# Joining the first pass's scatter with the second edge pass, in parts of 512 columns

## The chip, the cores and the metric

The kernel runs on one core of one Trainium2 chip. The metric is the device time of one execution in microseconds (us); lower is better.

## The reference

Four graph layers run one after another over the same 4096-node graph (`adj` 4096x4096, features 64 wide), each followed by a residual and a layer norm. The change touches the third, which runs the same layer twice (`it` 0 and 1):

```python
x = _layernorm(x + _L0_gnn_ref(x, adj, ...)); x = _layernorm(x + _L1_gnn_ref(x, adj, ...))
# third layer, twice, H = adj:
Q = x @ Wq + bq; V = x @ Wv + bv
edge_feat = H.T @ V                              # the "edge pass"
att = softmax(Q @ edge_feat.T * scale * H, axis=1)      # "attend"
...                                              # node and edge masks -> H_pruned
agg = (H_pruned.T * dv_isqrt[None, :] @ transformed) * de_inv[:, None]
msg = dv_isqrt[:, None] * (H_pruned @ agg)       # gather, then scatter
x   = relu(msg @ Theta)                          # the "messages"
# then a fourth layer with decaying weights
```

So the second pass begins with x = messages of the first: V = x @ Wv + bv needs them, and `H.T @ V` reads the whole matrix again.

## The kernel before

The matrix is handled as 32 row blocks of 128x4096 float32 (2048 KB). They stream from HBM into eight slots of on-chip memory (`slot`: six in `stream`, then `q2` and `x2`, which the trace calls query_twice and node_twice). All loads named here are issued by SyncE on one queue. Node features lie as [128, 32 blocks, 64]; a part is a quarter of that, 8 blocks or 512 columns.

The program is cut into phases by `phase(name)`. When a phase is left, all engines drain and meet (L172), GpSimd clears the phase's semaphores (L174), and all engines meet again (L175). Before the change there are two phases. `first_pass` holds `front` (the first two layers and the first edge pass), `attend` and `prune_and_sum` for it 0. `second_pass` holds `edge_pass`, `attend` and `prune_and_sum` for it 1, with the last layer.

`prune_and_sum` ends in eight groups of gather (L1658), aggregate (L1670) and scatter (L1686) on TensorE. After the last scatter, ScalarE (L1785) and VectorE (L1832) copy the sums from PSUM into `accT`, and TensorE makes the 32 messages (L1713) in two halves of 16, each over two parts; VectorE takes every part with relu and the node's factor (L1836). SyncE has meanwhile issued the loads of row blocks 0 to 7 of the next edge pass: two (L1613) and two (L1618) as slots fall free, and blocks 4 to 7 (L1621) when the scatter is done.

`edge_pass` then folds (transposes) all of x in 16 steps (L228), ScalarE copies the four parts back (L528), TensorE projects them by Wv (L215) and VectorE adds the bias (L534, `moved`). After that come the 32 edge blocks: block n is eight matmuls (L579) that add into PSUM banks 4 to 7. Between certain blocks stand other products (`beside`: features after block 6, queries after 9 and 11, and so on). SyncE reloads a place when its block was used (L554): block 8 goes where block 0 was, 9 where 1 was, 10 where 4 was, and from there six places take turns:

```python
def place(n):
    return n if n < 8 else (0, 1, 4, 5, 6, 7)[(n - 8) % 6]
```

`attend` copies the summed edge features out of PSUM (L1383 on VectorE, L1390 on ScalarE), then computes scores (L1140 on TensorE, L1175 on VectorE), exponentials on ScalarE and column sums (L1158). It begins when the semaphore of the last edge block says so, with no phase boundary ahead of it.

A matmul on float32 appears in the trace as two records, so an edge block of eight matmuls is 16 records.

Of the kernel before, what the change touches and what calls it, by code (L numbers as in the profile page):

```python
# [22 lines left out]
P = 128  # L23
# [65 lines left out]
def build(nc, d):  # L89
    ctx = ExitStack()  # L90
    with ctx:
# [417 lines left out]
        def edge_pass(block, sem, src, begun):  # L509
# [7 lines left out]
            features, query_first, query_second, _, _, fold_xn, nodes_first, nodes_second = side  # L517

            @block.tensor
            def _(pe):  # L520
                fold(src, fold4b, fold_ready)
                project(nat4, curT, wv, v_ready, before=lambda k: pe.wait_ge(fold_taken, k + 1))

            @block.scalar
            def _(act):
                for k in range(4):
                    act.wait_ge(fold_ready, k + 1)
                    nc.scalar.copy(bank_of(curT, k), bank_of(fold4b, k)).then_inc(fold_taken, 1)  # L528

            @block.vector  # L530
            def _(dve):
                for k in range(4):
                    dve.wait_ge(v_ready, k + 1)
                    nc.vector.tensor_tensor(part(moved, k), part(nat4, k), per_feature(bv, QB), ALU.add)\  # L534
                        .then_inc(v_taken, 1)
# [36 lines left out]

            return (used, NB)
# [115 lines left out]
        def front(block, sem):  # L689
# [390 lines left out]
            return (used, 4 * TILES + NB), (starts_stored, 16)  # L1080

# [281 lines left out]
        def attend(block, sem, it, edges_summed, edge_place_free):  # L1363
# [22 lines left out]
            def _(act):  # L1386
                for taken, value in (edges_summed, *edge_place_free):
                    act.wait_ge(taken, value)
# [4 lines left out]
            def _(sp):  # L1393
                sp.wait_ge(*edges_summed)
# [50 lines left out]
        def prune_and_sum(block, sem, it, scores_done, sums_done):  # L1445
# [108 lines left out]
            def place(n):  # L1554
                return (n + 8) % NB

# [67 lines left out]
            def _(pe):  # L1624
# [81 lines left out]

                pe.wait_ge(msg_taken, 4)
                for pair in ((24, 16), (0, 8)) if last_it else ((0, 8), (24, 16)):
                    for k in range(8):
                        for n in pair:  # L1710
                            h, m = divmod(place(n + k), 16)
                            at = 8 * TURN.index(n // 8) + k if last_it else n + k
# [183 lines left out]
```

## Time and profile before

| | |
|---|---|
| median of 3 runs | 2362.62 us (2361.77 to 2362.78) |
| the profiled execution, its own time | 2364.53 us |
| its span | 2362.6 us |
| mean granted TensorE clock | 0.944 of full |
| TensorE matmul busy | 2048.1 us (87%) |
| VectorE busy | 1727.4 us (73%) |
| ScalarE busy | 754.1 us (32%) |
| HBM traffic | 690.29 MB read, 136.31 MB written, 350 GB/s over the span |

The profiled execution's own time is 1.9 us over its span, and 1.9 us over the median of the runs. Times within the trace count from the start of the span. PEclk is the granted clock: 1.00 is 2.4 GHz, 0.50 is 1.2 GHz.

### The profile page before, as it was taken

The numbers are of one execution on the slowest core, as the hardware profiler recorded it, in microseconds if no ns is written. First come the engines' busy times: TensorE is split into PE (matmuls) and PEld (weight loads), VectorE is DVE, ScalarE is ACT, GpSimd is POOL, SyncE is SP. The second block draws the span as 40 slices with busy tenths as digits, with TensorE's granted clock in tenths as the row PEclk, the third lists the DMA queues.
The fourth block names the chain that finished last, engine by engine and source line by source line (L and its number), as shares of the span: only waits on it lengthen the run. The fifth ranks groups of instructions, "written<-read, shape, count | busy, mean of one in ns | idle before, by whom it ended". The sixth has DMA issues, their size and how long they took to land. (4 is left out here: it accounts for less than half of the span.)

```text
span 2362.6 us, 35866 instructions
## 1 busy us (share of the span) xinstructions
PE 2048.1 (87%) x15654; PEld 729.9 (31%) x15658; DVE 1727.4 (73%) x2056; ACT 754.1 (32%) x869; POOL 4.5 (0%) x18
## 2 busy tenths in 40 slices
PE   6899989899977777799999989987777689997997
PEld 2224333222322111234444323231212134344333
DVE  5996853188879999855541348879999965555998
ACT  0001000066634433211110026654433311112997
POOL 0000000000000000000000000000000000000000
PEclk9999999999988888799999999998888899998999
DMA  9988999999749999977779989938999987775994
GB/s 374 421 367 339 421 428 427 394 390 370 273 181 401 429 430 431 408 262 272 286 289 385 428 372 382 380 114 346 421 428 431 421 327 270 276 286 238 350 420 169
DMA packets 130219, 828.90 MB, mean 351 GB/s; under 512 B 8464, under 2 KB 10512, under 8 KB 76560
## 3 DMA queue, kind: packets, MB, share of 16 engines
q1 hardware_dynamic: 128016, 825.29, 86.7%
q8 instruction: 122, 2.00, 0.3%
q10 hardware_dynamic: 2048, 1.35, 0.2%
q14 instruction: 33, 0.27, 0.0%
HBM read 690.29 MB, written 136.31 MB: 350 GB/s over the span
## 5 line engine op out<-in xcount | busy, mean ns | idle before, releaser
L1185 ACT ACTIVATE stream<-stream,negmax 128x4096 f32<-128x4096 f32 x128 | 475.0, 3711 | 481.9 <-DVE negmax L1180 481.9
L1140 PE MATMUL ps<-edgeT,node_twice 64*128 64x512 f32 x1024 | 282.8, 672 | 156.3 <-DVE mx L1175 156.2
L1175 DVE CUSTOM_DVE_ANT_0 stream<-ps,stream 128x1024 f32<-128x1024 f32 x280 | 330.6, 1219 | 31.2 <-PE ps L1140 26.2
L1140 PE MATMUL ps<-edgeT,query_twice 64*128 64x512 f32 x1024 | 248.1, 616 | 4.3 <-DVE mx L1175 2.6
L579 PE MATMUL ps<-stream,moved_block 128*64 128x512 f32 x960 | 215.6, 597 | 27.8 <-DMA stream<-in_adj 27.8
L1686 PE MATMUL ps<-stream,xw 32*64 32x512 f32 x4096 | 227.5, 589 | 2.4 <-issue 1.8
L1140 PEld LDWEIGHTS ps<-edgeT,node_twice 64*128 64x128 f32 x1024 | 94.5, 201 | 342.5 <-DVE mx L1175 242.4
L1158 PE MATMUL ps<-stream,ones 128*1 128x512 f32 x1024 | 173.8, 813 | 9.3 <-DVE stream L1730 9.3
L1219 ACT ACTIVATE query_twice<-ps,less_one_exponent 128x512 int32<-128x512 int32 x256 | 154.9, 688 | 15.4 <-PE ps L1309 13.2
L1802 DVE STREAM_TRANSPOSE stream<-spare 128x4096 f32<-128x4096 f32 x22 | 97.5, 4432 | 72.1 <-PE ps L1686 51.2
L1686 PEld LDWEIGHTS ps<-stream,xw 32*64 32x64 f32 x4096 | 106.3, 132 | 121.3 <-issue 114.4
L1770 ACT COPY moved_block<-ps 128x512 f32<-128x512 f32 x16 | 9.4, 586 | 410.0 <-PE ps L1658 410.0
L1140 PEld LDWEIGHTS ps<-edgeT,query_twice 64*128 64x128 f32 x1024 | 87.6, 186 | 166.1 <-DVE mx L1175 104.0
L1802 DVE STREAM_TRANSPOSE stream<-query_twice 128x4096 f32<-128x4096 f32 x22 | 97.4, 4429 | 56.3 <-PE ps L1686 34.0
L1271 DVE SCALAR_TENSOR_TENSOR query_twice<-stream,query_twice 128x512 bf16<-128x512 f32 x216 | 131.6, 692 | 5.8 <-ACT query_twice L1219 5.8
L1802 DVE STREAM_TRANSPOSE stream<-node_twice 128x4096 f32<-128x4096 f32 x20 | 88.7, 4437 | 62.3 <-PE ps L1686 33.6
L1730 DVE SCALAR_TENSOR_TENSOR stream<-stream,cut 128x4096 f32<-128x4096 f32 x30 | 134.3, 4476 | 0.0
L1175 DVE CUSTOM_DVE_ANT_0 stream<-ps,moved_block 128x1024 f32<-128x1024 f32 x104 | 122.9, 1220 | 9.4 <-PE ps L1140 7.5
L1158 PE MATMUL ps<-stream,rz 128*1 128x512 f32 x1024 | 124.1, 604 | 6.1 <-DVE rz L1424 6.1
L579 PEld LDWEIGHTS ps<-stream,moved_block 128*64 128x64 f32 x960 | 65.5, 137 | 170.6 <-issue 116.4
L982 DVE SCALAR_TENSOR_TENSOR edgeT<-stream,edgeT 128x2048 bf16<-128x2048 f32 x46 | 105.4, 2292 | 8.4 <-DMA stream<-in_adjT 6.6
L1319 PE MATMUL ps<-query_twice,stream 128*64 128x512 bf16 x768 | 106.3, 385 | 5.6 <-DVE stream L1260 4.4
(233 smaller groups left out, 1959.8 us busy)
## 6 DMA issues: line engine op xcount, KB each, us to landing
stream<-in_adj SPq DMA_DIRECT2D x118, 2048.0 KB, 16.9
stream<-in_adjT SPq DMA_DIRECT2D x69, 2048.0 KB, 15.2
pruned<-stream SPq DMA_DIRECT2D x64, 2048.0 KB, 14.7
moved_block<-in_adj SPq DMA_DIRECT2D x24, 2048.0 KB, 14.5
spare<-pruned SPq DMA_DIRECT2D x22, 2048.0 KB, 11.4
query_twice<-pruned SPq DMA_DIRECT2D x22, 2048.0 KB, 11.5
node_twice<-pruned SPq DMA_DIRECT2D x20, 2048.0 KB, 11.4
spare<-in_adj SPq DMA_DIRECT2D x18, 2048.0 KB, 10.0
```

The costliest lines, as they stand in the source:

```text
L579: last = nc.tensor.matmul(ps[F * h:F * h + F, 4 + b, :], natural_block(moved, n), half_bank(src, b, h), start=n == 0, stop=n == NB - 1, sk ...
L982: step = v.scalar_tensor_tensor(out=counts, in0=src[:, e, :], scalar=0.0, in1=counts, op0=ALU.not_equal, op1=ALU.add)
L1140: last = nc.tensor.matmul(ps[:, 2 * slot + h, :], stationary[F * h:F * h + F, rows_n], bank_of(edgeT[F * h:F * h + F, :], c), start=True, ...
L1158: last = nc.tensor.matmul(ps[32 * g:32 * g + 1, 6 + half, :], w, bank_of(src, 4 * half + g), start=False, stop=False, skip_group_check=True)
L1175: nc.vector.tensor_tensor_reduce(out=out[:, cols], in0=ps[:, 2 * slot:2 * slot + 2, :].rearrange("p a b -> p (a b)"), in1=block_in[:, cols ...
L1185: nc.scalar.activation(out, out, ACT.Exp, bias=negmax[:, s:s + 1], accum_out=zsum[:, s:s + 1]).then_inc(exp_done, 1)
L1219: nc.scalar.activation(bank_of(clean, c).bitcast(I32), ps[:, c, :].bitcast(I32), ACT.Relu, bias=less_one_exponent[:, :], scale=1.0).then_i ...
L1271: v.scalar_tensor_tensor(out=bank_of(weight[u % 2], c), in0=bank_of(edges, c), scalar=0.0, in1=bank_of(clean, c), op0=ALU.not_equal, op1=A ...
L1319: last = nc.tensor.matmul(ps[F * h:F * h + F, 4 + 2 * half + q, :], natural_block(support[i], NB - 1 - k), bank_of(weight[u % 2], 2 * q + ...
L1686: last = nc.tensor.matmul(ps[F * h:F * h + F, q, :], agg[g % 2][r, b, :], src[r, :, b, :], start=g == 0 and b == 0, stop=g == groups - 1 a ...
L1730: nc.vector.scalar_tensor_tensor(out=kept, in0=kept, scalar=cut[:, s:s + 1], in1=buffer(t), op0=ALU.is_ge, op1=ALU.mult, accum_out=st["con ...
L1802: v.transpose(turned_pair[y % 3][:, N * (x % 2):N * (x % 2) + N], chunk_slot[x % 3])\
```

## The change

- The second edge pass moves out of `second_pass` into `first_pass`, behind `prune_and_sum` of it 0. `front` becomes a phase of its own. So the boundary between messages and folds goes, and there are two others: one between the first edge pass and the first `attend`, one between the second edge pass and the second `attend`. `attend`'s own waits for the edge sums go.
- The messages of it 0 are made in `edge_pass`, into PSUM banks 0 to 3 (`nat4`) and no longer into 4 to 7, so that edge blocks may start adding into 4 to 7 before all is taken.
- Ahead of edge block 0 stand all messages, but only part 0 of the folds and of the values. Parts 1 to 3 stand between the first blocks: a fold part (four transposes) after blocks 0, 2 and 4, a value part (four matmuls) after 1, 3 and 5. `features` moves from behind block 6 to behind block 7.
- VectorE takes message parts 0 and 1, then value part 0, then message parts 3 and 2, then value parts 1 to 3.

```diff
-        def edge_pass(block, sem, src, begun):
+        def edge_pass(block, sem, src, begun, msg_taken):
...
+            message_turn = (0, 1, 3, 2)
+            def messages(pair, ks):
+                for k in ks:
+                    for n in pair:
+                        last = message_product(nat4[:, n + k, :], n + k)
+                return last
+            def fold_part(pe, k):
+                pe.wait_ge(out_taken, message_turn.index(k) + 1)
+                for c in range(4 * k, 4 * k + 4):
+                    last = nc.tensor.transpose(fold4[:, P * c:P * c + P], pairs(src)[:, c, :], ident[:, :])
+                last.then_inc(fold_ready, 1)
+            def value_part(pe, k):
+                pe.wait_ge(fold_taken, k + 1)
+                for c in range(4 * k, 4 * k + 4):
+                    last = nc.tensor.matmul(pairs(nat4)[:, c, :], curT[:, P * c:P * c + P], wv[:, :],
+                                            start=True, stop=True)
+                last.then_inc(v_ready, 1)
             @block.tensor
             def _(pe):
-                fold(src, fold4b, fold_ready)
-                project(nat4, curT, wv, v_ready, before=lambda k: pe.wait_ge(fold_taken, k + 1))
+                pe.wait_ge(msg_taken, 4)
+                messages((0, 8), range(8)).then_inc(out_ready, 1)
+                fold_part(pe, 0)
+                messages((24, 16), range(4))
+                value_part(pe, 0)
+                messages((24, 16), range(4, 8)).then_inc(out_ready, 1)
...
+                message(0)
+                message(1)
+                take_value(0)
+                message(2)
+                message(3)
+                for k in (1, 2, 3):
+                    take_value(k)
                 vector(dve)
...
-                beside = {6: features, 9: query_first, 11: query_second, 20: fold_xn, 23: nodes_first,
+                beside = {0: lambda pe: fold_part(pe, 1), 1: lambda pe: value_part(pe, 1),
+                          2: lambda pe: fold_part(pe, 2), 3: lambda pe: value_part(pe, 2),
+                          4: lambda pe: fold_part(pe, 3), 5: lambda pe: value_part(pe, 3),
+                          7: features, 9: query_first, 11: query_second, 20: fold_xn, 23: nodes_first,
                           26: nodes_second}
-                pe.wait_ge(fold_taken, 4)
...
-        def attend(block, sem, it, edges_summed, edge_place_free):
+        def attend(block, sem, it):
...
-                for taken, value in (edges_summed, *edge_place_free):
-                    dve.wait_ge(taken, value)
...
-                sp.wait_ge(*edges_summed)
...
+        with phase("front") as (block, sem):
+            front(block, sem)
         with phase("first_pass") as (block, sem):
-            edges_summed, starts_kept_back = front(block, sem)
-            scores_done, sums_done = attend(block, of_stage(sem, "attend"), 0, edges_summed, (starts_kept_back,))
-            next_ahead = prune_and_sum(block, of_stage(sem, "prune"), 0, scores_done, sums_done)
+            scores_done, sums_done = attend(block, of_stage(sem, "attend"), 0)
+            next_ahead, msg_taken = prune_and_sum(block, of_stage(sem, "prune"), 0, scores_done, sums_done)
+            edge_pass(block, of_stage(sem, "edge"), cur, next_ahead, msg_taken)
         with phase("second_pass", next_ahead) as (block, sem):
-            edges_summed = edge_pass(block, sem, cur, next_ahead)
-            scores_done, sums_done = attend(block, of_stage(sem, "attend"), 1, edges_summed, ())
+            scores_done, sums_done = attend(block, of_stage(sem, "attend"), 1)
```

The change as it stands on TensorE, from the last scatter to the first edge blocks (line numbers of each kernel's own file). Before: messages, the boundary (L172), all folds, all values, edge blocks.

```order
L1686 MATMUL ps<-stream,xw 64x512 x128
L1713 MATMUL ps<-theta,accT 128x64 x32
L172 UNCONDITIONAL_BRANCH
L519 UNCONDITIONAL_BRANCH
L228 MATMUL ps<-ident,spare 128x128 x16
L215 MATMUL ps<-twice,moved_block 128x128 x16
L560 UNCONDITIONAL_BRANCH
L579 MATMUL ps<-stream,moved_block 64x512 x16
```

After: L516 are the messages, L542 the fold parts, L549 the value parts, L635 the edge blocks (eight matmuls each).

```order
L1732 MATMUL ps<-stream,xw 64x512 x128
L553 UNCONDITIONAL_BRANCH
L516 MATMUL ps<-theta,accT 128x64 x16
L542 MATMUL ps<-ident,spare 128x128 x4
L516 MATMUL ps<-theta,accT 128x64 x8
L549 MATMUL ps<-twice,moved_block 128x128 x4
L516 MATMUL ps<-theta,accT 128x64 x8
L616 UNCONDITIONAL_BRANCH
L635 MATMUL ps<-stream,moved_block 64x512 x8
L542 MATMUL ps<-ident,spare 128x128 x4
L635 MATMUL ps<-stream,moved_block 64x512 x8
L549 MATMUL ps<-twice,moved_block 128x128 x4
```

Twelve folds and twelve value matmuls moved from ahead of block 0 to between the first six blocks, and no phase boundary stands there any more.

On GpSimd the phase boundaries show (L172 with L174, which clears semaphores; L1149 and L1152 after, L1095 and L1098 before, are the reductions over all partitions in `prune_and_sum`). Before, from the last instructions of `front` to the second pass:

```order
L782 ISA per_partition<-per_partition 128x1
L1460 UNCONDITIONAL_BRANCH
L1095 ISA per_partition<-per_partition 128x1
L1098 ISA per_partition<-per_partition 128x1
L1786 UNCONDITIONAL_BRANCH
L1095 ISA per_partition<-per_partition 128x1
L1098 ISA per_partition<-per_partition 128x1
L172 UNCONDITIONAL_BRANCH
L174 ISA
```

After, the same stretch:

```order
L838 ISA per_partition<-per_partition 128x1
L172 UNCONDITIONAL_BRANCH
L174 ISA
L1509 UNCONDITIONAL_BRANCH
L1149 ISA per_partition<-per_partition 128x1
L1152 ISA per_partition<-per_partition 128x1
L1831 UNCONDITIONAL_BRANCH
L1149 ISA per_partition<-per_partition 128x1
L1152 ISA per_partition<-per_partition 128x1
L172 UNCONDITIONAL_BRANCH
L174 ISA x2
```

One boundary more stands in the program, behind `front`, and the one behind the first pass clears two ranges of semaphores where it cleared one.

## Rows read from the trace of the kernel before

**Rows 1.** The page: the span.

```profile
span 2362.6 us, 35866 instructions
```

**Rows 2.** Timeline, last scatter to first edge blocks: start us, us, engine, line, operation.

```profile
1239.20 1.29 DVE L1832 COPY accT<-ps 128x512 f32<-128x512 f32 x2 [19.18 <-PE ps L1686]
1240.54 5.43 PE L1713 MATMUL ps<-theta,accT 64*128 64x64 f32 x64 [1.40 <-DVE accT L1832]
1242.60 1.29 DVE L1836 SCALAR_TENSOR_TENSOR spare<-ps,dv 128x512 f32<-128x512 f32 x2 [2.11 <-PE ps L1713]
1246.02 1.29 DVE L1836 SCALAR_TENSOR_TENSOR spare<-ps,dv 128x512 f32<-128x512 f32 x2 [2.13 <-PE ps L1713]
1248.95 3.65 PE L228 MATMUL ps<-ident,spare 128*128 128x128 f32 x16 [2.98 <-PEq L175]
...
1252.63 0.59 ACT L528 COPY moved_block<-ps 128x512 f32<-128x512 f32 x1 [0.27 <-PE ps L228]
...
1256.18 6.23 PE L579 MATMUL ps<-stream,moved_block 128*64 128x512 f32 x28
```

**Rows 3.** Windows at that place; PEclk third from the end.

```profile
1242.60:1246.02 3.42, 3.38 (x32) 3.19 (x30) 1.29 (x3) 0.00 (x0) 0.00 (x0) 0.50 1.02 431
1248.95:1256.18 7.23, 7.23 (x48) 7.11 (x48) 2.08 (x3) 2.35 (x4) 0.00 (x0) 0.74 1.01 427
```

**Rows 4.** Loads of blocks 4 to 7: issue times, then us to landing.

```profile
L1621 SPq DMA_DIRECT2D stream<-in_adj x4: 328/429/803, 1239.2 to 1240.5; - x4
DMA to landing us min/median/max: 8.5/15.5/22.4
```

**Rows 5.** Reloads L554 of blocks 8, 10 and 31, each its issue and landing.

```profile
L554 SPq DMA_DIRECT2D stream<-in_adj x1: 327/327/327, 1259.9 to 1259.9; - x1
DMA to landing us min/median/max: 9.2/9.2/9.2
L554 SPq DMA_DIRECT2D stream<-in_adj x1: 328/328/328, 1273.6 to 1273.6; - x1
DMA to landing us min/median/max: 8.3/8.3/8.3
L554 SPq DMA_DIRECT2D stream<-in_adj x1: 328/328/328, 1359.8 to 1359.8; - x1
DMA to landing us min/median/max: 25.6/25.6/25.6
```

**Rows 6.** TensorE timeline of the edge pass, and its change to attend.

```profile
1280.37 3.84 PE L215 MATMUL ps<-twice,moved_block 128*128 128x128 f32 x32
...
1305.44 31.12 PE L579 MATMUL ps<-stream,moved_block 128*64 128x512 f32 x144
1336.49 1.97 PE L228 MATMUL ps<-ident,spare 128*128 128x128 f32 x16
...
1375.68 3.65 PE L579 MATMUL ps<-stream,moved_block 128*64 128x512 f32 x16 [1.24 <-DMA stream<-in_adj]
...
1385.47 3.65 PE L579 MATMUL ps<-stream,moved_block 128*64 128x512 f32 x16 [1.21 <-DMA stream<-in_adj]
1389.92 3.84 PE L1140 MATMUL ps<-edgeT,query_twice 64*128 64x512 f32 x16 [0.79 <-DVE edgeT L1383]
```

**Rows 7.** Timeline where attend of the first pass begins.

```profile
475.00 3.85 PE L1140 MATMUL ps<-edgeT,query_twice 64*128 64x512 f32 x16 [0.80 <-DVE edgeT L1383]
```

**Rows 8.** The semaphore clears L174: duration ns min/median/max, first and last start.

```profile
L174 POOLq EVENT_SEMAPHORE_RANGE_CLEAR  x3: 69/677/764, 1247.8 to 2362.2; - x3
```

**Rows 9.** Scores at the lower clock in prune, timeline and window; scores in attend.

```profile
706.69 2.08 PE L1140 MATMUL ps<-edgeT,node_twice 64*128 64x512 f32 x4 [3.51 <-DVE mx L1175]
706.66:710.08 3.42, 3.39 (x12) 0.76 (x16) 3.42 (x6) 0.00 (x0) 0.00 (x0) 0.52 0.94 383
1402.85 1.13 PE L1140 MATMUL ps<-edgeT,query_twice 64*128 64x512 f32 x4 [0.30 <-DVE mx L1175]
1402.71 1.22 DVE L1175 CUSTOM_DVE_ANT_0 stream<-ps,stream 128x1024 f32<-128x1024 f32 x1
```

More of the change, by code:

```diff
@@ L507, in edge_products, with node_place, message_product @@
             return vector, side, (make_starts(0), make_starts(1), roots), starts_stored
-        def edge_pass(block, sem, src, begun):
+        def node_place(n):
+            return (n + 8) % NB
+        def message_product(dst, n):
+            h, m = divmod(node_place(n), 16)
+            return nc.tensor.matmul(dst, accT[F * h:F * h + F, P * m:P * m + P], theta[F * h:F * h + F, :],
+                                    start=True, stop=True)
+        def edge_pass(block, sem, src, begun, msg_taken):
+            out_ready, out_taken = sem("message_ready"), sem("message_taken")
             fold_ready, fold_taken, v_ready, v_taken = (sem(n) for n in
@@ L527, in _, with message, take_value @@
                     act.wait_ge(fold_ready, k + 1)
-                    nc.scalar.copy(bank_of(curT, k), bank_of(fold4b, k)).then_inc(fold_taken, 1)
+                    nc.scalar.copy(bank_of(curT, k), bank_of(fold4, k)).then_inc(fold_taken, 1)
             @block.vector
             def _(dve):
-                for k in range(4):
-                    dve.wait_ge(v_ready, k + 1)
-                    nc.vector.tensor_tensor(part(moved, k), part(nat4, k), per_feature(bv, QB), ALU.add)\
-                        .then_inc(v_taken, 1)
+                v = nc.vector
+                def message(i):
+                    k = message_turn[i]
+                    dve.wait_ge(out_ready, i // 2 + 1)
+                    v.scalar_tensor_tensor(out=part(src, k), in0=part(nat4, k), scalar=0.0,
+                                           in1=per_node_part(st["dv"], k), op0=ALU.max, op1=ALU.mult)\
+                        .then_inc(out_taken, 1)
+                def take_value(k):
+                    dve.wait_ge(v_ready, k + 1)
+                    v.tensor_tensor(part(moved, k), part(nat4, k), per_feature(bv, QB), ALU.add).then_inc(v_taken, 1)
+                message(0)
[5 more added lines that the diff above has]
+                    take_value(k)
                 vector(dve)
@@ L571, in _ @@
                         beside[n](pe)
-            return (used, NB)
         def edge_block(n, src):
@@ L1078, in _ @@
                 edge_vector(dve)
-            return (used, 4 * TILES + NB), (starts_stored, 16)
         def global_softmax_vector(dve, do, sems):
@@ L1386, in _ @@
             def _(act):
-                for taken, value in (edges_summed, *edge_place_free):
-                    act.wait_ge(taken, value)
                 for k in (2, 3):
@@ L1552, in first_row @@
                 return (24 + 8 * c) % NB
-            def place(n):
-                return (n + 8) % NB
             def buffer(t):
@@ L1705, in _ @@
                 scatter(groups - 1)
+                if not last_it:
+                    return
                 pe.wait_ge(msg_taken, 4)
-                for pair in ((24, 16), (0, 8)) if last_it else ((0, 8), (24, 16)):
+                for pair in ((24, 16), (0, 8)):
                     for k in range(8):
                         for n in pair:
-                            h, m = divmod(place(n + k), 16)
-                            at = 8 * TURN.index(n // 8) + k if last_it else n + k
-                            last = nc.tensor.matmul(nat4b[:, at, :], accT[F * h:F * h + F, P * m:P * m + P],
-                                                    theta[F * h:F * h + F, :], start=True, stop=True)
+                            last = message_product(nat4b[:, 8 * TURN.index(n // 8) + k, :], n + k)
                     last.then_inc(out_ready, 1)
@@ L1835, in message @@
                     dve.wait_ge(out_ready, i // 2 + 1)
-                    return v.scalar_tensor_tensor(out=part(cur, k), in0=part(nat4b, i if last_it else k), scalar=0.0,
+                    return v.scalar_tensor_tensor(out=part(cur, k), in0=part(nat4b, i), scalar=0.0,
                                                   in1=per_node_part(st["dv"], k), op0=ALU.max, op1=ALU.mult)
                 if not last_it:
-                    for i, k in enumerate((0, 1, 3, 2)):
-                        message(i, k).then_inc(out_taken, 1)
                     return
```

3 lines of the change are left out of this document (2 added, 1 removed).

## The prediction

> **What bounds the kernel now.** I read the page first, then the chain of waits, then the timeline from the last scatter of the first pass to the second `attend`, and at the end the landings of the reloads there. The span is 2362.6 us [rows 1]; its own time is 2364.53, so 1.9 lies around it, and the median of the runs shown, 2362.62, is 1.9 under that own time. I make the sum against the own time and take off 1.9 at the end.
>
> The place that the change rebuilds is short. The sums are copied from 1239.20; messages begin at 1240.54, VectorE ends the last of them at 1246.02 + 1.29 = 1247.31, folds begin at 1248.95 and edge block 0 at 1256.18 [rows 2]. So 17 us pass between the end of the scatter and the first edge block, part of them at the lower clock (0.50, 1.2 GHz, from 1242.6 on) [rows 3].
>
> What the reader should see next is that those 17 us are not idle time of the kernel's tightest resource. Blocks 4 to 7 are issued at 1239.2 to 1240.5; the first lands 8.5 later, at 1247.7, the last 22.4 later, at 1262.9 [rows 4]. Near the end of the pass TensorE waits over 1.2 us for each block, and its blocks start at 1375.68 and 1385.47, that is 4.89 apart for a block [rows 6]; TensorE itself needs only (1336.49 - 1305.44) / 9 = 3.45 [rows 6]. 2048 KB in 4.89 us is what the queue gives when it is full. The end of the pass is the landing of block 31, 1359.8 + 25.6 = 1385.4 [rows 5], and 3.65 of matmuls behind it [rows 6]. With no gap, 24 loads behind the landing at 1262.9 would end at 1262.9 + 24 x 4.89 = 1380.3. **The stream of loads has 5.1 us of gaps in it, and no more than that can come back here**, however early block 0 starts. Where they are: block 8 is issued at 1259.9 and lands at 1269.1, block 10 is issued at 1273.6 and lands 8.3 later at 1281.9 [rows 5]. Without gaps these would be 1267.8 and 1262.9 + 3 x 4.89 = 1277.6, so 1.3 are lost by block 8 and 4.3 in all by block 10. Block 10 goes where block 4 was, and so waits until block 4 is used.
>
> **The change part by part.** Early start. Ahead of block 0 are now the first messages, to 1242.60 [rows 2], one message part (0.69 of the 1.29 for two, to 1243.3), a fold part and, after half of the other messages, a value part. At the lower clock 16 folds took 3.65 against 1.97 at the full one [rows 2, 6], so four take 0.9: to 1244.2. ScalarE's copy of 0.59 [rows 2] lies beside the next eight messages. The second 16 messages took from 1242.60 to 1246.0, 3.4 for 16 [rows 2, 3], so eight take 1.7: to 1245.9. The value part, like a fold part, 0.9: to 1246.8; its bias 0.7 on VectorE lies beside the last eight messages, 1.7: to 1248.5. Block 0 starts there, 7.7 earlier. It begins at the lower clock. A block at half the clock costs up to 3.45 more; before, the clock came back while folds and values ran (0.74 on the mean from 1248.95 to 1256.18 [rows 3]), so I take it to come back within block 0 and price this at 1.5, between 0 and 3.4.
>
> Block 4 is then used after five blocks of 3.45, four parts of 0.5 (a quarter of 1.97 [rows 6]), and 0.2 for the end of the pipeline and the issue: 1248.5 + 1.5 + 17.2 + 2.0 + 0.2 = 1269.4. The reload of block 10 issued then, with the 8.3 that a load alone took [rows 5], lands at 1277.7, just where the stream without gaps has it (1277.6). Block 8 is issued at about 1253.6 and queues behind block 7, block 9 at 1257.6 likewise. The later reloads have room: features (3.84 [rows 6]) now stand behind block 7, so block 8 is used at 1269.4 + 4 x 3.45 + 3.84 + 2 x 0.5 = 1288.0 and the reload of block 14 alone would land at 1296.3, where the full stream has it at 1262.9 + 7 x 4.89 = 1297.1. I leave 0.5 for gaps that remain, since block 8 before took 9.2 and not 8.3 though the queue had only just run empty [rows 5]. **Gain: 5.1 - 0.5 = 4.6**; block 31 lands at 1380.8. Its ends: 5.1, and 1.6 if block 4 is used 3 us later than reckoned.
>
> The parts between the blocks cost 6 x 0.5 = 3 us of TensorE, and the 1.2 us waits for loads at the end of the pass hide them; were that cover gone, they would count in full, but then they took the place of the same work ahead of block 0. On VectorE value parts 1 to 3 are queued ahead of the copy that waits for `features`, all of them done by block 6. Message parts 3 and 2 wait for the last messages; what is queued behind them on VectorE, value part 1, is needed by edge block 8 only. SyncE's queue has no new wait.
>
> Boundaries. The one between messages and folds cost 1248.95 - 1247.31 = 1.64 [rows 2]; it goes, but this was already in the gain above, since the gain is counted from the loads. Two are added on the path: `attend` begins 0.80 after the first edge pass's last block, and 0.79 after the second's [rows 6, 7], with nothing between. Each now has drains, a clear and two meetings ahead of the copies of the edge sums. The row for this is the same 1.64, of which a clear is 0.68 to 0.76, with 0.07 for a small second range [rows 8]; the front alone has fewer semaphores, the first pass now two ranges. I take **2 x 1.65 = 3.3**, ends 2.4 and 4.0. Nothing hides them: TensorE, VectorE and ScalarE all wait, and the loads of `attend` are issued later too.
>
> Clock. TensorE's gap before the scores grows from 0.8 to 2.45 us. After a gap of 3.51 the scores of a chunk took 2.08 at a granted 0.52, against 1.13 at 1.00, and VectorE takes a chunk in 1.22 [rows 9]. In the first block of four chunks that is up to 4 x (2.08 - 1.22) = 3.4 us at one boundary if the whole block is slow, and 0 if the clock holds, as it did over the gaps of 0.8 [rows 6, 7]. The gap of 1.4 ahead of the messages [rows 2] was followed by 0.50 [rows 3]. 2.45 lies between 1.4 and 3.5, both followed by the lower clock, but the messages are short matmuls, so the first is a weak witness. I take one of the two boundaries to lose a third of its price: **1.2**. The Trainium skill (Perfetto Trace Analysis, Matmul Optimizations) says that the matmul engine scales with its use and that matmuls should run back to back; by that rule the two new gaps are a harm which the change's own purpose doesn't show, and at full price for both the sum would be 5.6 worse. The trace agrees in kind (0.52 after the 3.51 gap [rows 9]).
>
> **Sum:** 2364.53 - 4.6 + 3.3 + 1.2 = 2364.4 own time, less 1.9: **2362.5** at the median. A measurement of this kernel tells about 0.2%, 4.7 us, from no change.
>
> **The rivals.**
> (a) The clock holds over both new gaps: -4.6 + 3.3 = -1.3, 2361.3. For it: the scores came right behind blocks with gaps of 1.2 and one of 0.8 and still took the 3.84 of the full clock [rows 6]. Against it: the gap is twice as long.
> (b) The low clock is dear at both boundaries, 2 x 2.6 (each three quarters of 3.4): -4.6 + 3.3 + 5.2 = +3.9, 2366.5.
> (c) Slower than before: the lower clock lasts past block 0, because the first blocks start sooner after the short messages than they did. From block 4 used at 1269.4 on, each us late is one us lost. Two whole blocks at half the clock cost 6.9 instead of 1.5, block 4 is used 5.4 later, and the gain is 4.6 - 5.4 = -0.8; with the forecast's costs the sum is +5.3, 2367.9. From block 4 at 1270.7 on, the gain is under the 3.3 of the boundaries alone, and the change is a loss whatever else happens. Against it: before, the clock was back while folds and values ran, which are less dense than edge blocks [rows 3].
> (d) The loads aren't the bound, and the pass ends as much earlier as it begins: -7.7 + 3.3 + 1.2 = -3.2, and with clock held and a start of 9 earlier -5.7, 2356.9. The Trainium skill (Perfetto Trace Analysis, Optimization Strategy) advises interleaving stages that have different busiest engines, which is what the parts do; its promise is this case. Against it stand the waits of over 1.2 us for each of the last blocks [rows 6] and a landing 25.6 after its issue, 17.3 more than alone [rows 5]: the queue is the bound.
>
> **How the numbers follow.** Forecast 0.43, (a) 0.25, (b) 0.14, (c) 0.09, (d) 0.09. 2362.5 is the likeliest. The range reaches down past (a) to a full gain with cheap boundaries (-5.1 + 2.4 = -2.7: 2359.9) and up to the lower part of (b), 2366.0; what is left out is under 0.2. Faster by over 0.2% needs (d) at its far end, 0.05; slower by over 0.2% needs (b) or (c) beyond their price, 0.05; the rest, 0.90, is within.
>
> **What would show it.** Edge block 0 of the second pass 7 to 8 us earlier after the scatter; the landings of blocks 8 to 31 spaced 4.9 with no window under 300 GB/s between the issue of block 4 and that of `attend`; block 31 landed 141.6 after the first of those issues where it was 146.2; a gap of 2.4 us on TensorE ahead of both `attend` stages; a granted clock of 0.5 right behind one of them. Wrong if block 10 still leaves a hole in the stream, if a boundary costs over 2.5, or if `attend` as a whole gets longer than by that gap.

## The result, and the profile after

| | before | after |
|---|---|---|
| median of 20 runs each | 2362.22 us (2358.42 to 2365.4) | 2366.17 us (2361.1 to 2372.25) |
| ratio | | 1.0019, 95% interval 1.0012 to 1.0026 |
| span of the profiled execution | 2362.6 us | 2365.2 us |

The changed kernel is about 4.4 us slower on the mean of the runs (2366.28 against 2361.89, from which the ratio comes), 4.0 by the medians. The forecast was no change, 2362.5, in a range that ends at 2366.0; the time lies just over it, and the change is a small loss where the forecast had none.

The timeline of TensorE, VectorE and SyncE after the last scatter (L516 messages, L542 fold parts, L549 value parts, L635 edge blocks, L576 message parts taken):

```profile
1241.05 1.29 DVE L1877 COPY accT<-ps 128x512 f32<-128x512 f32 x2 [19.16 <-PE ps L1732]
1242.40 2.35 PE L516 MATMUL ps<-theta,accT 64*128 64x64 f32 x32 [1.41 <-DVE accT L1877]
1245.55 1.11 PE L542 MATMUL ps<-ident,spare 128*128 128x128 f32 x4 [0.80 <-DVE spare L576]
1246.59 1.97 PE L516 MATMUL ps<-theta,accT 64*128 64x64 f32 x16
1248.50 2.07 PE L549 MATMUL ps<-twice,moved_block 128*128 128x128 f32 x8
1250.50 1.97 PE L516 MATMUL ps<-theta,accT 64*128 64x64 f32 x16
1252.40 6.18 PE L635 MATMUL ps<-stream,moved_block 128*64 128x512 f32 x16
1258.52 0.66 PE L542 MATMUL ps<-ident,spare 128*128 128x128 f32 x4
1259.10 3.65 PE L635 MATMUL ps<-stream,moved_block 128*64 128x512 f32 x16
1262.69 1.16 PE L549 MATMUL ps<-twice,moved_block 128*128 128x128 f32 x8
```

I count everything here from the copy of the sums (1239.20 before [rows 2], 1241.05 after). Block 0 now starts at 11.35 for 16.98, so 5.6 earlier. But it takes 6.18 and not 3.65, and a fold and a value part stand behind it and the next ones. A value part is 1.16 at the full clock and 2.07 at the lower one.

Windows of the same stretch, the granted clock third from the end:

```profile
1244.30:1252.40 8.10, 7.30 (x50) 6.33 (x48) 1.98 (x3) 0.58 (x1) 0.00 (x0) 0.50 1.00 427
1252.40:1258.50 6.10, 6.10 (x18) 1.62 (x16) 1.29 (x2) 0.00 (x0) 0.00 (x0) 0.58 1.00 424
1277.00:1279.00 2.00, 2.00 (x12) 0.59 (x10) 0.00 (x0) 0.48 (x1) 0.00 (x0) 1.00 0.95 197
```

The lower clock holds from the middle of the first messages through the first fold and value part and nearly all of block 0. In the last window only 197 GB/s move: the hole in the stream of loads is still there. The reload of block 10 and that of block 31, each with its landing:

```profile
L610 SPq DMA_DIRECT2D stream<-in_adj x1: 327/327/327, 1276.3 to 1276.3; - x1
DMA to landing us min/median/max: 8.7/8.7/8.7
L610 SPq DMA_DIRECT2D stream<-in_adj x1: 328/328/328, 1362.7 to 1362.7; - x1
DMA to landing us min/median/max: 26.1/26.1/26.1
```

Block 10 is issued at 35.2 for 34.4 before [rows 5], later and not earlier. The last block lands at 147.7 for 146.2, and TensorE starts it as soon as it is there. The two places where `attend` begins (timeline):

```profile
475.05 1.29 DVE L1435 COPY edgeT<-ps 128x512 f32<-128x512 f32 x2 [17.32 <-PEq L175]
475.80 1.13 PE L1194 MATMUL ps<-edgeT,query_twice 64*128 64x512 f32 x4 [1.89 <-DVE edgeT L1435]
...
1388.87 3.65 PE L635 MATMUL ps<-stream,moved_block 128*64 128x512 f32 x16 [1.22 <-DMA stream<-in_adj]
1394.78 3.84 PE L1194 MATMUL ps<-edgeT,query_twice 64*128 64x512 f32 x16 [2.25 <-DVE edgeT L1435]
```

TensorE's gaps are 1.89 and 2.25 for 0.8 [rows 6, 7]. So the traces show +1.5 in the edge pass, +1.1 and +1.5 at the boundaries, 4.1 together, about what the ratio says. The other stages differ between any two executions by 1 to 2 us each, up and down (the span itself grew by only 2.6 here), so from here on I read stages in the trace and use the ratio for the whole.

### The profile page after: what moved, and what is told of

Read it like the earlier page. It is cut to its first block and busy times, and to the rows that moved or that the text cites. A ratio compares the mean times of both kernels' runs of the same rounds, so it can differ in the third digit from the quotient of the medians.

```text
span 2365.2 us, 35892 instructions
## 1 busy us (share of the span) xinstructions
PE 2052.6 (87%) x15658; PEld 724.7 (31%) x15658; DVE 1726.8 (73%) x2056; ACT 753.8 (32%) x869; POOL 4.5 (0%) x18
## 5 line engine op out<-in xcount | busy, mean ns | idle before, releaser
L635 PE MATMUL ps<-stream,moved_block 128*64 128x512 f32 x960 | 219.8, 607 | 25.0 <-DMA stream<-in_adj 25.0
L1273 ACT ACTIVATE query_twice<-ps,less_one_exponent 128x512 int32<-128x512 int32 x256 | 154.8, 687 | 14.8 <-PE ps L1363 12.4
L1732 PEld LDWEIGHTS ps<-stream,xw 32*64 32x64 f32 x4096 | 101.1, 132 | 126.9 <-issue 124.5
L635 PEld LDWEIGHTS ps<-stream,moved_block 128*64 128x64 f32 x960 | 66.3, 139 | 168.1 <-issue 119.6
## 6 DMA issues: line engine op xcount, KB each, us to landing
pruned<-stream SPq DMA_DIRECT2D x64, 2048.0 KB, 14.7
```

Source lines behind the costliest of these rows:

```text
L635: last = nc.tensor.matmul(ps[F * h:F * h + F, 4 + b, :], natural_block(moved, n), half_bank(src, b, h), start=n == 0, stop=n == NB - 1, sk ...
L1273: nc.scalar.activation(bank_of(clean, c).bitcast(I32), ps[:, c, :].bitcast(I32), ACT.Relu, bias=less_one_exponent[:, :], scale=1.0).then_i ...
L1732: last = nc.tensor.matmul(ps[F * h:F * h + F, q, :], agg[g % 2][r, b, :], src[r, :, b, :], start=g == 0 and b == 0, stop=g == groups - 1 a ...
```

## The experiments

**Theory 1**: the second edge pass ends when its loads end, the stream of loads has one hole that counts, ahead of block 10, and that hole is as long as block 4 is used late. The parts between the first blocks, with the lower clock, make block 4 late; the boundaries are a fixed price. **Rivals**: the boundaries (or the joining) cost more than their gaps; or TensorE's own work, not the loads, sets the pass.

What the runs gave, times in us from the copy of the sums to: the start of block 0, the issue of block 10's reload, the start of the last block.

| kernel | block 0 | reload of 10 | last block | ratio to before (95%) |
|---|---|---|---|---|
| before | 16.98 | 34.4 | 146.3 | |
| after | 11.35 | 35.2 | 147.8 | 1.0019 (1.0012 to 1.0026) |
| e1 boundary behind front | 18.4 | 35.8 | 147.5 | 1.0002 (0.9993 to 1.0011) |
| e10 boundary behind edge pass | 16.98 | 34.4 | 146.2 | 1.0001 (0.9992 to 1.0010) |
| e8 parts alone | 14.7 | 38.7 | 151.6 | 1.0019 (1.0010 to 1.0028) |
| e7 joining alone | 13.8 | 31.2 | 142.9 | 1.0003 (0.9992 to 1.0013) |
| e3 late parts | 11.1 | 29.6 | 142.9 | 0.9998 (0.9989 to 1.0007) |
| e4 third place, on before | 15.2 | 25.8 | 143.2 | 0.9995 (0.9986 to 1.0004) |
| e5 third place, on after | 7.9 | 20.5 | 141.2 | 1.0001 (0.9993 to 1.0010) |
| e6 both, on after | 11.35 | 24.4 | 142.0 | 0.9995 (0.9986 to 1.0004) |
| e9 both, on before | 14.3 | 26.1 | 143.8 | 0.9992 (0.9982 to 1.0002) |
| e11 twelve matmuls | 8.2 | 29.6 | 142.3 | 1.0018 (1.0009 to 1.0026) |
| e13 ten matmuls | 7.9 | 29.3 | 142.6 | 1.0017 (1.0008 to 1.0026) |
| e12 eight matmuls | 7.9 | 29.3 | 142.4 | 1.0012 (1.0003 to 1.0021) |
| e14 twelve elsewhere | 11.3 | 35.2 | 147.6 | 1.0036 (1.0022 to 1.0050) |

**The boundaries, one at a time.** On the kernel before:

```diff
+        with phase("front") as (block, sem):
+            front(block, sem)
         with phase("first_pass") as (block, sem):
-            edges_summed, starts_kept_back = front(block, sem)
-            scores_done, sums_done = attend(block, of_stage(sem, "attend"), 0, edges_summed, (starts_kept_back,))
+            scores_done, sums_done = attend(block, of_stage(sem, "attend"), 0, None, ())
```

> The kernel before with one edit: front is a phase of its own, so that a boundary stands between the first edge pass and the first attend. Theory 1 (each boundary is a fixed price and the edge pass is bound by its loads): the gap from the end of the last edge block to the first scores goes from 0.8 to 1.9 us, as it did with the whole change (473.90 to 475.80), and the time rises by about 1.1 us, ratio 1.0005. Rival (the boundary also costs behind the gap, through the clock or late loads of attend): the 32 blocks of attend take longer too, 2 to 4 us in all, ratio 1.001 to 1.002.

```diff
-        with phase("second_pass", next_ahead) as (block, sem):
-            edges_summed = edge_pass(block, sem, cur, next_ahead)
-            scores_done, sums_done = attend(block, of_stage(sem, "attend"), 1, edges_summed, ())
+        with phase("edge", next_ahead) as (block, sem):
+            edge_pass(block, sem, cur, next_ahead)
+        with phase("second_pass") as (block, sem):
+            scores_done, sums_done = attend(block, of_stage(sem, "attend"), 1, None, ())
```

> The kernel before with one edit: a boundary between the second edge pass and the second attend, in a phase of its own; the boundary ahead of the folds stays. Theory 1: the gap ahead of the second attend goes from 0.8 to 1.9 to 2.3 us and the time rises by 1.1 to 1.5, ratio 1.0005. It clears only the few semaphores of the edge pass, so 1.1 is likelier than 1.5. Rival: as for the front's boundary, more than the gap, ratio 1.001 to 1.002.

The gaps came out at 1.89 and 1.79 for 0.80 and 0.79, so 1.1 and 1.0 each, and the ratios are 1.0002 and 1.0001, within their intervals the same as the gaps. The intervals end at 1.0011 and 1.0010, so up to 2.6 us for one boundary isn't excluded, but neither is the loss of 1.0019. In the profiled execution of e1 the boundary did cost more than its gap. The clock fell to 0.50 for 3.4 us right behind it, and the first scores took 5.40 for 3.85 [rows 7]:

```profile
474.88 5.40 PE L1140 MATMUL ps<-edgeT,query_twice 64*128 64x512 f32 x16 [1.89 <-DVE edgeT L1383]
```

The second edge pass of e1 wasn't edited, yet block 10's reload came at 35.8 and the last block started at 147.5, 1.2 later than before: the lower clock lasted until 1257.3 there, half way through the values, and block 0 began at 18.4. A version of the changed kernel without its two new boundaries wasn't tried.

**The parts alone.** The kernel before with its boundaries, and only the parts between the blocks:

```diff
             @block.tensor
             def _(pe):
-                fold(src, fold4b, fold_ready)
-                project(nat4, curT, wv, v_ready, before=lambda k: pe.wait_ge(fold_taken, k + 1))
+                fold_part(pe, 0)
+                value_part(pe, 0)
...
-                beside = {6: features, 9: query_first, 11: query_second, 20: fold_xn, 23: nodes_first,
+                beside = {0: lambda pe: fold_part(pe, 1), 1: lambda pe: value_part(pe, 1),
+                          2: lambda pe: fold_part(pe, 2), 3: lambda pe: value_part(pe, 2),
+                          4: lambda pe: fold_part(pe, 3), 5: lambda pe: value_part(pe, 3),
+                          7: features, 9: query_first, 11: query_second, 20: fold_xn, 23: nodes_first,
```

> The kernel before with only the parts: fold part 0 and value part 0 ahead of edge block 0, parts 1 to 3 between the first six blocks, features behind block 7, the boundaries as they were. Block 0 starts about 3 us earlier (1253.3 for 1256.18), but block 4 now has 2 x 0.6 + 2 x 1.1 = 3.4 us of parts ahead of its end and may have a slow block 0 too. Theory 1 (the reload of block 10 waits for block 4, and the loads bound the pass): block 4 is used 0.5 to 3 us later than before and the pass ends 0 to 3 us later, ratio 1.000 to 1.0013. Rival (the pass ends as much earlier as it begins): 3 us less, ratio 0.9987.

The reload of block 10 and the last block of this kernel:

```profile
L568 SPq DMA_DIRECT2D stream<-in_adj x1: 328/328/328, 1277.9 to 1277.9; - x1
DMA to landing us min/median/max: 8.6/8.6/8.6
```

```profile
1390.77 3.65 PE L595 MATMUL ps<-stream,moved_block 128*64 128x512 f32 x16 [1.22 <-DMA stream<-in_adj]
```

Block 0 starts 2.2 earlier than before, the reload of block 10 is issued 4.3 later (38.7), and the last block starts 5.3 later. The ratio is 1.0019, as large as with the whole change, and this kernel has neither the joining nor the new boundaries. This speaks against both rivals and for theory 1, with a size over what I expected (0 to 3 us): in this execution the lower clock held 17 us.

**The joining alone.** The changed kernel with all messages, folds and values ahead of block 0:

```diff
                 messages((0, 8), range(8)).then_inc(out_ready, 1)
-                fold_part(pe, 0)
-                messages((24, 16), range(4))
-                value_part(pe, 0)
-                messages((24, 16), range(4, 8)).then_inc(out_ready, 1)
+                messages((24, 16), range(8)).then_inc(out_ready, 1)
+                for k in range(4):
+                    fold_part(pe, k)
+                for k in range(4):
+                    value_part(pe, k)
```

> The changed kernel with nothing between the edge blocks: joined, but all messages, then all folds, then all values, ahead of block 0, and features behind block 6. So it is the joining alone, with its three boundaries. Theory 1: one boundary of 1.6 us less ahead of block 0, which starts at 15 to 16 us for 16.98 before; block 4 is used at 33 for 34.4 and the last block starts at about 145 for 146.3; with the two new boundaries (1.1 and 1.0 to 1.5) the sum is +1 us against before, ratio 1.000 to 1.001. Rival (joining itself does harm, the parts do not): ratio 1.0019 as in the changed kernel.

Last block at 142.9, 3.4 earlier than before, and ratio 1.0003: what the joining wins in the edge pass, the boundaries take. So the joining does no harm by itself. Block 0 starts 2.4 later than in the changed kernel while the last block starts 5 earlier: the start of block 0 alone doesn't tell the end.

**Later parts.** On the changed kernel:

```diff
-                beside = {0: lambda pe: fold_part(pe, 1), 1: lambda pe: value_part(pe, 1),
-                          2: lambda pe: fold_part(pe, 2), 3: lambda pe: value_part(pe, 2),
-                          4: lambda pe: fold_part(pe, 3), 5: lambda pe: value_part(pe, 3),
-                          7: features, 9: query_first, 11: query_second, 20: fold_xn, 23: nodes_first,
+                beside = {4: lambda pe: fold_part(pe, 1), 5: lambda pe: value_part(pe, 1),
+                          6: lambda pe: fold_part(pe, 2), 8: lambda pe: value_part(pe, 2),
+                          9: lambda pe: fold_part(pe, 3), 10: lambda pe: value_part(pe, 3),
+                          12: features, 14: query_first, 16: query_second, 20: fold_xn, 23: nodes_first,
```

> The changed kernel with its parts later: fold and value parts 1 to 3 behind edge blocks 4, 5, 6, 8, 9 and 10, features behind 12, queries behind 14 and 16. Blocks 0 to 4 follow each other with nothing between. All times from the copy of the scatter's sums. Theory 1 (the reload of block 10 waits for block 4): that reload is issued at 31.6 us for 35.2 in the changed kernel, lands at about 40 for 44.0, and the last block starts at 144.3 for 147.8; the scores begin 3.5 us earlier than in the changed kernel, ratio to before 1.000 to 1.001. Rival (the added waits or the short low-clock start set the pass): as in the changed kernel, 147.8, ratio 1.0019.

```profile
L610 SPq DMA_DIRECT2D stream<-in_adj x1: 328/328/328, 1268.0 to 1268.0; - x1
DMA to landing us min/median/max: 8.5/8.5/8.5
```

```profile
1381.26 3.65 PE L635 MATMUL ps<-stream,moved_block 128*64 128x512 f32 x16 [1.22 <-DMA stream<-in_adj]
```

The same work on TensorE, only behind block 4 (features and queries move back too): the reload at 29.6 (31.6 expected), the last block at 142.9 (144.3), the ratio 0.9998 for 1.0019.

**Another place for block 10.** The place of block 2 is free until the nodes are written there behind block 23, so it can take one more load:

```diff
-                return n if n < 8 else (0, 1, 4, 5, 6, 7)[(n - 8) % 6]
+                return n if n < 8 else 2 if n == 10 else (0, 1, 4, 5, 6, 7)[(n - 8 - (n > 10)) % 6]
...
-            seq = [*((28, 29, 26, 27) if last_it else (26, 27, 28, 29)), 30, 31, *range(26)]
+            seq = [*((29, 30, 27, 28, 26, 31) if last_it else (26, 27, 28, 29, 30, 31)), *range(26)]
```

> The kernel before with another turn of places: block 10 goes where block 2 was and not where block 4 was, and the six places take turns one block later; attend's order of blocks follows, so that its first three are still at hand. Theory 1 (the stream of loads has a gap because block 10 waits for block 4): reload of block 10 is issued at 1266.7 for 1273.6 and lands at 1278.9 for 1281.9, the last block lands 3 to 4 us earlier and the time falls by as much, ratio 0.9985. Rival (TensorE's own work or the chain on VectorE bounds the pass): no change, ratio 1.000.

> The changed kernel with block 10 in the place of block 2 (as the same turn of places on the kernel before). Theory 1: the reload of block 10 is issued at 26.4 for 35.2 and queues behind block 9's, so it lands at 38.1 for 44.0; block 15's is the next that is just late; the last block starts at 142 to 143 for 147.8, 5 us less than the changed kernel, ratio to before 0.9995 to 1.000. Rival: TensorE's parts and not the loads set the pass: 147 to 148, ratio 1.0019.

The reload of block 10 on the kernel before, then on the changed one, with the last block and the scores of the latter:

```profile
L554 SPq DMA_DIRECT2D node_twice<-in_adj x1: 328/328/328, 1266.6 to 1266.6; - x1
DMA to landing us min/median/max: 12.4/12.4/12.4
```

```profile
L610 SPq DMA_DIRECT2D node_twice<-in_adj x1: 328/328/328, 1260.3 to 1260.3; - x1
DMA to landing us min/median/max: 17.8/17.8/17.8
```

```profile
1380.99 3.65 PE L635 MATMUL ps<-stream,moved_block 128*64 128x512 f32 x16 [1.22 <-DMA stream<-in_adj]
1386.90 5.40 PE L1194 MATMUL ps<-edgeT,query_twice 64*128 64x512 f32 x16 [2.25 <-DVE edgeT L1435]
```

12.4 and 17.8 us to landing for 8.3 alone [rows 5]: the load now queues, as it should. On the kernel before, the last block starts 3.0 earlier (143.2); the expected ratio of 0.9985 was too bold, since 0.9995 leaves 3 us less inside its interval but doesn't show it. On the changed kernel all 24 reloads land 4.9 apart, and the last block starts at 141.2; that is what a stream without holes gives. The parts stand there where the change puts them, so TensorE's work isn't what sets the pass. In this execution the clock didn't fall at the messages (block 0 at 7.9), but it fell behind the boundary: the first scores took 5.40 for 3.84. The ratio of 1.0001 is less good than the trace gives: 5.1 us won in the pass and 2.6 paid at the boundaries would be 2.5 less than before, 0.9989, outside the interval (0.9993 to 1.0010). Where the rest went stays open.

Both repairs together, on the changed kernel and on the one before (with the parts, but not joined):

> The changed kernel with both repairs, late parts and block 10 in the place of block 2. Each alone already gave a stream with almost no gap (last block at 142.9 and 141.2), so theory 1 expects no more than 141.2 to 142 for both, not the sum of the two gains; scores at 147, ratio 0.9995 to 1.0005, about 2 us over the version without joining because of the two boundaries. Rival (the two gains are of different kinds and add): last block at 136 to 138.

> The kernel before (its two boundaries) with the parts late (behind blocks 4 to 10, features behind 12) and block 10 in the place of block 2. No joining. Theory 1: block 0 starts 2 us earlier than before, the reloads of blocks 8 to 10 queue without a gap, the last block starts at 141.2 to 143 us after the copy of the sums (before 146.3, parts alone 151.6), the scores at 145.7 to 147.5 (before 150.7), and nothing is paid for boundaries: ratio 0.998 to 0.999. If the parts cost by themselves wherever they stand, the last block starts at 148 or later and the ratio is over 1.001.

The last block starts at 142.0 and 143.8: the two gains don't add. Both remove the same hole, and now something else sets the end. In the first of the two:

```profile
L610 SPq DMA_DIRECT2D stream<-in_adj x1: 328/328/328, 1362.6 to 1362.6; - x1
DMA to landing us min/median/max: 18.1/18.1/18.1
```

```profile
1341.17 1.97 PE L228 MATMUL ps<-ident,spare 128*128 128x128 f32 x16 [1.38 <-DVE spare L441]
...
1367.81 17.39 PE L635 MATMUL ps<-stream,moved_block 128*64 128x512 f32 x80
```

The load of block 31 lands at 1380.7, 141.1 after the copy, but TensorE runs the last five blocks one after another without a wait and starts the last one 0.9 later. It waited 1.38 for VectorE ahead of a fold instead, which the kernel with the third place alone does not. In the other kernel with both repairs it is the same, with 0.4 for 0.9. So there TensorE's own work sets the end, by a small margin. 2360.63 and 2360.49 us against 2362.0 for the kernel before are the two best medians of this study, but both intervals include 1. No version that is clearly faster came of it.

**The clock.** On the changed kernel, with `keep_busy(n)` issuing n bf16 matmuls of zeros (128x512) into PSUM bank 7, which the first edge block overwrites:

```diff
+                keep_busy(6)
                 pe.wait_ge(msg_taken, 4)
                 messages((0, 8), range(8)).then_inc(out_ready, 1)
+                keep_busy(4)
                 fold_part(pe, 0)
                 messages((24, 16), range(4))
+                keep_busy(2)
                 value_part(pe, 0)
```

> The changed kernel with twelve bf16 matmuls of 128x512 zeros added on TensorE into an unused PSUM bank: six while it waits for the copy of the sums, four while it waits for the first message part, two ahead of the value part. They change no result. If the lower clock at the start is what makes block 4 late: messages, value part and block 0 take 2.1, 1.2 and 3.65 for 3.9, 2.1 and 6.2, block 4 is used at 30 for 35.2, and the last block starts at 142 to 143 for 147.8, ratio to before 1.000. If the added matmuls do not keep the clock, they add 0.5 to 1 us and the rest is as in the changed kernel, ratio 1.002.

Timeline of this kernel (L556 are the added matmuls, L643 edge blocks), and one window of it, granted clock third from the end:

```profile
1239.19 1.47 PE L556 MATMUL ps<-zeros_b 128*128 128x512 bf16 x6
1240.67 2.00 PE L516 MATMUL ps<-theta,accT 64*128 64x64 f32 x32
...
1245.54 1.05 PE L549 MATMUL ps<-twice,moved_block 128*128 128x128 f32 x8
...
1247.56 3.65 PE L643 MATMUL ps<-stream,moved_block 128*64 128x512 f32 x16
```

```profile
1244.00:1246.00 2.00, 2.00 (x25) 1.74 (x24) 0.01 (x1) 0.59 (x1) 0.00 (x0) 1.00 0.99 426
```

The clock stays at 1.00, the value part takes 1.05 and block 0 3.65, the reload of block 10 is issued at 29.6 for 35.2 and the last block starts at 142.3 for 147.8. The edge pass is as expected, but the ratio of 1.0018 is not. The trace shows where the time went: from the first scatter of the second pass to its messages, 229.5 us in the changed kernel and in the one before, this kernel takes 234.0, with three groups at 31.4 to 31.6 for 30.6 and the last scatter at 18.8 for 16.9. Three more runs asked why:

> The changed kernel with eight added bf16 matmuls (five while TensorE waits for the copy, three while it waits for the first message part) where the first try had twelve. In the first try the edge pass was 5.5 us shorter, but the scatters of the second pass had every other group at 31.5 us for 30.6, and the time was no better. If that comes from where the code lies, which the number of added instructions shifts, then with eight the groups are all 30.6 again, the last block starts at 142 to 143, and the ratio is about 1.000. If keeping the clock up early itself costs later, the groups are again at 31.5 and the ratio 1.0018.

> As with eight, but ten added matmuls (six and four): the same edge pass as with twelve within 0.5 us. If where the code lies decides the groups of the second pass's scatter, ten may fall either way and the time goes with it: 1.000 with groups at 30.6, 1.0015 or more with groups at 31.5. If the clock decides, it is as with twelve.

Eight and ten matmuls in place of twelve: 233.5 and 234.2, ratios 1.0012 and 1.0017. My hope that eight would fall well was wrong. So the same twelve at a place where they keep no clock, behind edge block 20:

```diff
+                else:
+                    for _ in range(12):
+                        nc.tensor.matmul(ps[:, 0, :], zeros_b[:, 0:P], zeros_b[:, :], start=True, stop=True)
                 fold(tmp, fold4).then_inc(xn_folded, 1)
```

> The changed kernel with the same twelve bf16 matmuls of zeros, but behind edge block 20 of the second edge pass, ahead of the fold of xn, where TensorE is ahead of its loads. They take about 2.6 us there and are hidden, since the pass ends with TensorE waiting for loads; the last block starts at 147 to 149 as in the changed kernel. If the longer program makes the scatters of the second pass slow: first scatter to messages 233 to 234 us for 229.5, groups at 31.5, and the ratio to before is 1.003 to 1.004. If it is the early clock: 229.5, groups at 30.6, ratio 1.002.

One scatter of the second pass in this kernel, then in the changed one:

```profile
1959.87 14.94 PE L1735 MATMUL ps<-stream,xw 32*64 32x512 f32 x256
```

```profile
1961.02 13.99 PE L1732 MATMUL ps<-stream,xw 32*64 32x512 f32 x256
```

234.3 us again, ratio 1.0036. So the slow scatters come with the added instructions wherever they stand, and not with the clock. Of two kernels with the same twelve, the one that keeps the clock (1.0018) is faster by 0.0018, 4.3 us, than the one that does not (1.0036), next to the 5.3 us by which its last block starts earlier. The ratios alone hardly part them (five runs of e14, and the intervals meet at 1.0022 to 1.0026), but the traces do: with the added matmuls ahead of and between the messages the clock stayed up in three profiled executions of three, and without them it fell between the scatter and the edge blocks in eleven of twelve. The lower clock at the start was a real part of the loss.

## Why the prediction was wrong

- **The bound was read rightly.** The last block starts 111.7 to 113.3 us after block 10's reload is issued, in every kernel where that load lands 8.2 to 9.1 after its issue (all but e4, e5, e6 and e9). Issued still earlier, it queues behind other loads and the distance grows (117.4 in e4, 120.7 in e5), and a stream without holes puts the last block at 141.2, 5.1 under before. That is the 5.1 that the prediction allowed. It didn't see how little lies under that bound: in e6 and e9 TensorE's own work ended the pass.
- **The step that failed** is the use of block 4, put at 1269.4 - 1239.2 = 30.2 after the copy and measured at 35.2, 5 late. **The term most at fault** is "The value part, like a fold part, 0.9" and, between the blocks, "four parts of 0.5". The rows had the right number: 16 value matmuls take 3.84 at the full clock, as the row for `features` shows, which are the same kind [rows 6], so a part is 1.0 and not 0.5, and about 2 at the lower clock. Measured from start to start: 1.09 and 2.00. The three value parts ahead of block 4's end are 2.3 of the 5. The fold parts, 0.59 and 1.04 for 0.5 and 0.9, are 0.3.
- **The same step's other term**, 1.5 for the clock in block 0, measured 6.18 - 3.65 = 2.5, so 1.0 more. It was inside its range, yet I took the range's cheap half.
- The rest of the 5, about 1.4, lies in small seams. The first messages with the wait behind them ended at 4.5 for 4.1, and each later eight took 1.9 for 1.7. An edge block with a part behind it takes 3.59 from start to start and not 3.45. So block 0 started at 11.35 and not at 1248.5 - 1239.2 = 9.3, of which the first value part is 1.1.
- By the prediction's own rule that each us late is one us lost, the gain of 4.6 becomes a loss of 0.4. The other 1.1 of the measured loss of 1.5 came behind the issue: the load took 8.7 for 8.3, and from its landing to that of block 31 the stream took 103.8 for the 103.1 of the sum. Rival (c) had the rule and the limit (block 4 from 1270.7 on), with 0.09; it gave the low clock as the only cause and not the value parts.
- **The boundaries** cost 1.1 and 1.5, not 1.65 each. The clock didn't fall behind them in the profiled execution. Over all traces with such gaps (1.8 to 2.25 us) it fell behind six of twenty: behind the first in e1 and e12, behind the second in e3, e5, e11 and e13. The first 16 scores then took 5.40 for 3.84, and that `attend` 196.0 to 197.1 us for 193.0 to 196.1 in the others. Six in twenty at 1.6 each, two boundaries to a kernel, is 0.9 us on the average, so 1.2 was a fair price, though not one that each execution pays.
- The range ended at 2366.0 and the median is 2366.17. What put it outside was the pass, 6.1 worse than forecast (+1.5 for -4.6); the boundaries and the clock behind them came 1.9 cheaper than their 3.3 + 1.2, which hid part of it.
- The rule of the Trainium skill (Perfetto Trace Analysis, Matmul Optimizations) that matmuls should run back to back, was weighed only for the boundaries. The clock mattered more at the messages: e11 against e14 puts it at 4.3 us there. The rule tells only half of that case, since the wait of 1.4 stood ahead of the messages but they themselves ran without a gap when the clock fell. Its other rule (the Trainium skill, Perfetto Trace Analysis, Optimization Strategy), to interleave stages with different busiest engines, gave nothing here, since the work was put ahead of the very block for which the loads waited.

## What to carry to other kernels

Where loads bound a stage, ask which use of a buffer frees the next one, and put no other work ahead of that use; work of the same size four to five blocks later cost nothing that shows here. Then look at the next bound: in e6 TensorE's own work ended the pass, 0.9 us behind the loads. The early start of a stage is worth nothing by itself. Price a part of a step from a row of the same operation, since on TensorE a float32 projection took nearly twice a transpose of the same tile.

## What the runs showed of the hardware

- Eight to twelve more instructions in TensorE's program before the second pass made its scatters (2 x 16 x 4 matmuls on 32 rows in a group) slower: two or three groups of eight at 31.3 to 31.6 us for 30.6, and the last scatter at 18.8 to 19.3 for 16.2 to 18.3, 4 to 5 us in all, in four kernels out of four, with nothing else changed there. Why is not shown. That the weight loads wait on the way to the engine, because the program lies otherwise, is an argument; the trace gives these waits no releaser.
- The clock fell between the scatter and the edge blocks in eleven of twelve executions without added matmuls, for 3.4 us (e4) to 17 (e8), and not in e5, with the same program ahead of it. Between e5 and the changed kernel that alone moves block 0 by 3.5 us. In the kernel before it stayed low through messages that kept TensorE busy 3.38 of 3.42 us [rows 3]. The spread of the runs goes with the clock: of the 20 runs of the changed kernel the fastest, 2361.1 us, had a mean granted clock of 0.946 and the slowest, 2372.25, 0.939.
- Behind a gap of 0.8 us on TensorE ahead of `attend` the clock fell in none of ten cases, behind one of 1.8 to 2.25 in six of twenty.
- A reload issued when the queue was empty or had under 0.5 us left landed after 8.3 to 8.8 us, in a full one 4.9 after the one before it. A few landings in most kernels came 5.3 to 6.5 us after the one before although the queue was full (before: 57.4 to 63.2). Their cause stays open; they are 1 to 3 us of a pass.
